# An LSTM with its weights made stationary: gates by units instead of rows, and the input part accumulated in PSUM

## The reference

```python
xW = jnp.einsum('ntd,dk->tnk', x, Wx) + b
c0 = jnp.zeros_like(h0)
def step(carry, xw_t):
    prev_h, prev_c = carry
    a = xw_t + prev_h @ Wh
    i = jax.nn.sigmoid(a[:, 0:Hdim])
    f = jax.nn.sigmoid(a[:, Hdim:2 * Hdim])
    o = jax.nn.sigmoid(a[:, 2 * Hdim:3 * Hdim])
    g = jnp.tanh(a[:, 3 * Hdim:4 * Hdim])
    next_c = f * prev_c + i * g
    next_h = o * jnp.tanh(next_c)
    return ((next_h, next_c), next_h)
_, hs = jax.lax.scan(step, (h0, c0), xW)
return x + jnp.transpose(hs, (1, 0, 2))
```

## Time and profile before

| | us |
|---|---|
| median of 3 runs | 1101.32 (1098.41 to 1105.87) |
| the profiled execution | 1104.56 |
| its span, from first to last instruction | 1102.8 |
| VectorE busy | 790.9 (72%) |
| TensorE products busy | 701.9 (64%) |
| TensorE weight loads busy | 578.7 (52%) |
| ScalarE busy | 550.2 (50%) |

### The profile page before, as it was taken

One profiled execution on the slowest core, in us unless ns is written; L12 is line 12 of the kernel. 1 busy time (PEld: TensorE's weight loads), 2 busy tenths in 40 slices (PEclk: granted clock), 3 DMA queues, 4 the chain that ended last, 5 costly groups with the idle time before them and its releaser, 6 DMA issues.

```text
span 1102.8 us, 88125 instructions
## 1 busy us (share of the span) xinstructions
PE 701.9 (64%) x36864; PEld 578.7 (52%) x36864; DVE 790.9 (72%) x4897; ACT 550.2 (50%) x3586; POOL 0.7 (0%) x6
## 2 busy tenths in 40 slices
PE   1766666666666666666666666666666666666664
PEld 1555555555555555545555555555555555555554
DVE  2676777777777767777767777777777777777776
ACT  0454555545555545555545555555555555455544
POOL 0000000000000000000000000000000000000000
PEclk9998999989999989999989999999999999899989
DMA  2000000000000000000000000000000000000000
GB/s 85 6 6 6 5 7 6 6 6 6 6 6 6 6 6 5 6 7 6 6 7 5 6 6 6 6 6 6 6 6 5 7 6 6 6 6 6 6 6 7
DMA packets 31869, 8.73 MB, mean 8 GB/s; under 512 B 31344, under 2 KB 31344, under 8 KB 31856
## 3 DMA queue, kind: packets, MB, share of 16 engines
q1 hardware_dynamic: 31248, 8.41, 3.2%
q10 hardware_dynamic: 608, 0.14, 0.1%
HBM read 6.43 MB, written 2.10 MB: 8 GB/s over the span
## 4 chain that ended last, share of the span: by engine, by line
DVE 50%; PE 25%; ACT 14%; issue 8%; DMA 2%; DVEq 1%; SPq 0%
DVE turned_bank L295 38%; PE gates L363 25%; DVE h_pad L313 8%; ACT tanh_o L211 8%; ACT turned_bank L214 6%; DVE scan_both L300 3%; DMA wh_raw<-in_L_cond_Wh_dram 2%; DVEq L329 1%; DVE cell L306 1%; DVE h_rows L269 0%; SPq L142 0%; SPq L137 0%; DVEq L268 0%; DVE wh L224 0%; DVE wh L221 0%
## 5 line engine op out<-in xcount | busy, mean ns | idle before, releaser
L363 PE MATMUL gates<-wh,h_pad 128*32 128x64 f32 x32768 | 594.7, 227 | 374.8 <-DVE h_pad L313 371.0
L363 PEld LDWEIGHTS gates<-wh,h_pad 128*32 128x32 f32 x32768 | 509.8, 114 | 489.1 <-DVE h_pad L313 485.1
L295 DVE STREAM_TRANSPOSE turned_bank<-gates 128x64 f32<-128x64 f32 x2048 | 478.5, 262 | 184.0 <-PE gates L363 170.8
L202 ACT ACTIVATE tanh_f<-turned_bank 128x8 f32<-128x8 f32 x512 | 90.7, 177 | 449.1 <-DVE turned_bank L295 417.5
L209 ACT ACTIVATE scan_both<-turned_bank 128x8 f32<-128x8 f32 x1024 | 185.1, 181 | 61.1 <-DVE turned_bank L295 19.7
L313 DVE SCALAR_TENSOR_TENSOR h_pad<-tanh_o,turned_bank 128x4 f32<-128x4 f32 x1024 | 132.8, 158 | 74.4 <-ACT turned_bank L214 5.2
L306 DVE TENSOR_TENSOR_SCAN cell<-scan_both 128x12 f32<-128x12 f32 x1024 | 143.8, 181 | 1.9 <-issue 0.3
L214 ACT ACTIVATE turned_bank<-cell 128x4 f32<-128x4 f32 x1024 | 143.3, 172 | 2.3 <-DVE cell L306 0.3
L345 PE MATMUL x_acc<-wx,x_units 128*32 128x128 f32 x2048 | 108.8, 287 | 16.6 <-DVE x_units L248 16.6
L211 ACT ACTIVATE tanh_o<-turned_bank 128x8 f32<-128x8 f32 x512 | 90.7, 177 | 29.2 <-DVE turned_bank L295 7.0
L215 ACT ACTIVATE half_d<-cell 128x8 f32<-128x8 f32 x512 | 100.4, 196 | 0.0
(11 more groups left out here) (24 smaller groups left out, 6.7 us busy)
## 6 DMA issues: line engine op xcount, KB each, us to landing
x_next<-in_x_dram SPq DMA_DIRECT2D x256, 8.0 KB
x_here<-in_x_dram SPq DMA_DIRECT2D x256, 8.0 KB
out_dram<-y_rows SPq DMA_DIRECT2D x256, 8.0 KB
wx_raw<-in_L_cond_Wx_dram SPq DMA_DIRECT2D x2, 512.0 KB
wh_raw<-in_L_cond_Wh_dram SPq DMA_DIRECT2D x2, 512.0 KB
bias_raw<-in_L_cond_b_dram ACTq DMA_DIRECT2D x4, 32.0 KB, 3.5
h_rows<-in_cond_dram ACTq DMA_DIRECT2D x4, 1.0 KB
```

The source lines that it names most:

```text
L202: nc.scalar.activation(tanh_f[:], of_step(BF, t), ACT.Tanh).then_inc(tanh_f_done, 1)
L295: nc.vector.transpose(turned[k], gates[k][:, 0:W]).then_inc(gates_turned[k], 1)
L363: last = nc.tensor.matmul(gates[k][q * R:(q + 1) * R, 0:W], h_stationary(b, t), wh[:, b, q, columns_of(k)], start=False, stop=b == M - 1, ...
```

## The change

The operands change places: the weights are stationary, 32 columns at a time, and the 4 columns of h move. A product's result has 32 units of one gate, half and quadrant as its partitions and the sequences as its columns. So the gates come out with units as partitions, the turns of the gate banks and the permuted copies of the weights are gone, and ScalarE reads the gate banks directly. A bank of one step consists of two parts (`PARTS`), each with its own stationary tiles.

The input part and the bias are written straight to the gate banks. There are two sets of four banks, each for 4 steps (`SET`). After the products of each step TensorE fills one bank of the other set: for each of the bank's two parts 4 products of the bias row with ones and 8 of `wx` with 16 columns of `x_units` (`x_part`). `x_acc`, `x_part` (the tile), `inject` and the identity go. The turn of the next `x` moves from step 2 to step 4 and waits for `x_used`. `tanh_c` moves from PSUM to SBUF. `BA`'s half 0 is now issued ahead of the wait for `h_done[1]`.

```diff
+    PARTS = (((F, 0), (F, 1)), ((G, 0), (I, 0)), ((G, 1), (I, 1)), ((O, 0), (O, 1)))
...
-        gates = [ps(f"gates{k}", [128, 512]) for k in BANKS]
-        x_acc = ps("x_acc", [128, 512])
-        turned_bank = [ps(f"turned_bank{k}", [128, 512]) for k in range(3)]
+        gates = [[ps(f"gates{s}{k}", [128, 512]) for k in range(len(PARTS))] for s in range(SETS)]
...
+        def group(t, k):
+
+            at = t % SET * N
+            return gates[t // SET][k][:, 0:2 * SC].rearrange("p (g c) -> p g c", g=2)[:, :, at:at + N]
...
-                    act.wait_ge(gates_turned[BF], now)
-                    nc.scalar.activation(tanh_f[:], of_step(BF, t), ACT.Tanh).then_inc(tanh_f_done, 1)
+                    act.wait_ge(gates_done[BF], now)
+                    nc.scalar.activation(tanh_f[:], group(t, BF), ACT.Tanh).then_inc(tanh_f_done, 1)
...
-                if ahead and t == 2:
-
+                if ahead and t == SET:
+                    dve.wait_ge(x_used, chunk + 1)
                     dve.wait_ge(x_next_loaded, (chunk + 2) * (Q * DMA))
                     nc.vector.transpose(x_units[:], x_next[:]).then_inc(x_turned, 1)
-                if ahead and t == STEPS - 1:
-                    make_x_part(chunk + 1)
-
-                def turn(k):
-                    dve.wait_ge(gates_done[k], now)
-                    nc.vector.transpose(turned[k], gates[k][:, 0:W]).then_inc(gates_turned[k], 1)
...
-                turn(BF)
-                turn(BA)
-                turn(BB)
                 forget()
-                turn(BO)
                 update(0)
                 update(1)
                 hidden(0)
...
+            def weights(w, b, gate, m, q):
+                at = gate * D + q * QD + m * R
+                return w[:, b, at:at + R]
+
+            def x_part(k, s):
+
+                for g, (gate, m) in enumerate(PARTS[k]):
+                    where = slice(g * SC, (g + 1) * SC)
+                    for q in range(Q):
+                        at = gate * D + q * QD + m * R
+                        nc.tensor.matmul(gates[s][k][q * R:(q + 1) * R, where], bias_row[:, at:at + R], ones[:],
+                                         start=g == 0, stop=False, tile_position=(0, q * R), skip_group_check=True)
+                    for b in range(M):
+                        for q in range(Q):
+                            last = nc.tensor.matmul(gates[s][k][q * R:(q + 1) * R, where], weights(wx, b, gate, m, q),
+                                                    x_units[:, b * R + s * SC:b * R + (s + 1) * SC],
+                                                    start=False, stop=False, tile_position=(0, q * R), skip_group_check=True)
+                return last
...
-                def recur(b, k):
-                    for q in range(Q):
-                        last = nc.tensor.matmul(gates[k][q * R:(q + 1) * R, 0:W], h_stationary(b, t),
-                                                wh[:, b, q, columns_of(k)], start=False, stop=b == M - 1,
-                                                tile_position=(0, q * R), skip_group_check=True)
+                def recur(b, k, parts=(0, 1)):
+                    for g in parts:
+                        gate, m = PARTS[k][g]
+                        for q in range(Q):
+                            last = nc.tensor.matmul(group(t, k)[q * R:(q + 1) * R, g, :], weights(wh, b, gate, m, q),
+                                                    h_units[:, b, (t - 1) % STEPS, :], start=False, stop=b == M - 1,
+                                                    tile_position=(0, q * R), skip_group_check=True)
                     return last
 
                 pe.wait_ge(h_done[0], now)
                 recur(0, BF)
+                recur(0, BA)
                 pe.wait_ge(h_done[1], now)
                 recur(1, BF).then_inc(gates_done[BF], 1)
...
+                recur(1, BA).then_inc(gates_done[BA], 1)
+                recur(0, BB)
+                recur(1, BB).then_inc(gates_done[BB], 1)
+                recur(0, BO)
+                recur(1, BO).then_inc(gates_done[BO], 1)
+                k, s = t % SET, (t // SET + 1) % SETS
+                if s == 1:
+                    last = x_part(k, 1)
+                    if k == SET - 1:
+                        last.then_inc(x_used, 1)
+                elif ahead:
+                    if k == 0:
+                        pe.wait_ge(x_turned, chunk + 2)
+                    x_part(k, 0)
```

More of the change, by code:

```diff
@@ L62, in lstm_residual_kernel @@
         x_here = sb("x_here", [128, QD])
-        x_part = sb("x_part", [128, GC])
         tanh_f = sb("tanh_f", [128, M, N])
         tanh_o = sb("tanh_o", [128, M, N])
+        tanh_c = [sb(f"tanh_c{m}", [128, N]) for m in range(M)]
         half_d = sb("half_d", [128, M, N])
@@ L102, in lstm_residual_kernel @@
         y_stored = sem("y_stored")
[L104 to L105 removed]
+        gates_done = [sem(f"gates_done{k}") for k in range(len(PARTS))]
         tanh_f_done = sem("tanh_f_done")
@@ L190, in _, with cell_tanh @@
                 act.dma_start(h0_rows[q * R:q * R + N, :], cond[:, q * QD:(q + 1) * QD]).then_inc(h0_loaded, DMA)
+            act.wait_ge(bias_zeroed, 1)
+            act.dma_start(bias_row[0:1, :], bias.rearrange("(a c) -> a c", a=1)).then_inc(bias_loaded, DMA)
             nc.scalar.activation(table_probe[:, 1:2], table_probe[:, 0:1], ACT.Tanh)
             act.wait_ge(zeroed, 2)
-            def of_step(k, t):
-                return turned[k].rearrange("p (g c) -> p g c", g=M)[:, :, t * N:(t + 1) * N]
+            def cell_tanh(m, now):
+                act.wait_ge(cell_done[m], now)
+                nc.scalar.activation(tanh_c[m][:], cell[:, m, :, K - 1], ACT.Tanh, scale=0.5).then_inc(tanh_done[m], 1)
             with act.Fori(0, T, STEPS) as t0:
@@ L218, in _, with scale_weights @@
         def _(dve):
[L219 to L228, removed]
+            def scale_weights(w, b, factor, loaded):
                 dve.wait_ge(loaded[b], DMA)
[L230 to L234, removed]
+                if factor != 1.0:
+                    nc.vector.tensor_scalar(w[:, b, G * D:], w[:, b, G * D:], factor, None, ALU.mult)
+                return nc.vector.tensor_scalar(w[:, b, 0:G * D], w[:, b, 0:G * D], 0.5 * factor, None, ALU.mult)
             nc.vector.memset(table_probe[:], 0.0)
@@ L338, in _ @@
         def _(pe):
-            def x_product(b, columns, chunk):
-                opens = (b, columns) == PIECES[0]
-                if opens:
-                    pe.wait_ge(x_turned, chunk + 1)
-                for q in range(Q):
-                    last = nc.tensor.matmul(x_acc[q * R:(q + 1) * R, columns], x_units[:, b * R:(b + 1) * R],
-                                            wx[:, b, q, columns], start=opens, stop=b == M - 1,
-                                            tile_position=(0, q * R), skip_group_check=True)
-                if (b, columns) == PIECES[-1]:
-                    last.then_inc(x_acc_done, 1)
@@ L351, in inject @@
-            def inject(k):
-                for q in range(Q):
-                    nc.tensor.matmul(gates[k][q * R:(q + 1) * R, 0:W], ident[:, q * R:(q + 1) * R],
-                                     x_part[:, columns_of(k)], start=True, stop=False,
-                                     tile_position=(0, q * R), skip_group_check=True)
+            def weights(w, b, gate, m, q):
[8 more added lines that the diff above has]
+                                         start=g == 0, stop=False, tile_position=(0, q * R), skip_group_check=True)
+                    for b in range(M):
+                        for q in range(Q):
[3 more added lines that the diff above has]
+                return last
```

119 lines of the change are left out of this document (39 added, 80 removed).

## The result

| | before | after |
|---|---|---|
| median, us | 1103.59 (4 runs, 1098.41 to 1109.97) | 2991.81 (4 runs, 2983.74 to 2998.10) |
| span of the profiled execution, us | 1102.8 | 2996.1 |

The changed kernel takes 2.7105 times as long (95% interval 2.6999 to 2.721). The forecast was 1715 us, with a range of 1000 to 1860: the direction and the mechanism were right, the size was far off.

The account below looks back on a forecast made before the run. Bound now: a serial recurrence, half the span VectorE. After: instruction fetches, 63 passes of 26.4 us (1663), last 8 steps 21, start 27, end 3: 1714, corrected to 1713, forecast 1715 us; range 1000 to 1860, its own 1420 to 1920.

Parts of the forecast that it names:

- What bounds the kernel, and what goes.: Whole kernel: a serial recurrence, half the span VectorE; all 2048 gate-bank turns, 478.5 us of VectorE, leave.
- I take 7 ns; the bounds are 6.7 and 14.: TensorE's 4-column products: time per load-and-multiply pair, taken from eight loads after a wait.
- At the 1.2 GHz level a product of 4 columns loses little, 10 us in all: TensorE's stretches at low clock: they were to add only 10 us to the changed kernel's time.
- 128r + 0.79: One recurrence step in us, r the time per pair: 1.69 us at 7 ns, 2.58 at 14.
- Rival 3: Recurrence products: no fetch trouble, but small products don't go below 14 ns; 1350 us, chance 0.18.
- 2070 us: Recurrence products: about 25 ns from product to product, 4 us a step; chance 0.03 within the 14 ns rival's.
- The body doesn't fit, and is fetched packet by packet, one ahead.: TensorE's loop: 2816 instructions, 11 packets, exceed its instruction memory; each packet is requested when the previous one is entered.
- A packet costs 2.2 us from request to arrival (bounds 1.84 and 2.9).: TensorE's instruction fetch: 1.2 us to the packet's start plus 0.96 us transfer; 11 packets make 24.2 us for 8 steps.
- today TensorE takes 4 us for 256 instructions, which hides it: Kernel before: executing one packet's instructions takes 4 us, longer than the 2.2 us claimed for a fetch.
- The jump back waits once more: End of TensorE's loop body: its target packet has been overwritten, adding 2.2 us, 26.4 us a pass.
- Rival 1: TensorE's loop: memory holds the whole body, or fetches run far enough ahead never to show; 900 us, chance 0.12.
- rival 2: TensorE's loop: fetches overlap, 0.96 us a packet, only the jump back waits 2.2 us; 1040 us, chance 0.18.

Follow-up runs that it names:

- the four-step body: Changed kernel's stationary weights with TensorE's loop body 4 steps instead of 8, whole computation kept: 1351.53 us, 1.2189 times before.
- the padded kernels: Kernel before with 16, 24 or 38 unread products a step added behind steps 0 to 6: 1360.32, 2089.16 and 2515.46 us.
- the two kernels with half of the contraction: Changed kernel without contraction half 0 in the recurrence: 2020.43 us; also without it in the x part, and without the bias: 988.91 us.
- the first three with fillers: Kernel with 4-step loop body plus unread products behind each step: 4 or 8 of 128 columns, or 8 of 256: 1278.00, 1206.96, 1404.81 us.

## Why the prediction was wrong in size and right in kind

- **What bounds the kernel, and what goes.** Right. The turns left VectorE, and its busy time fell by 338 us.
- **"I take 7 ns; the bounds are 6.7 and 14."** The value was wrong, the bound right: 13.4 ns in the changed kernel. I took it from the eight loads of the earlier trace rows. Their starts end at 504.29, and the ninth comes 53 ns later (the line below), so that row says nothing of the pace beyond eight, and I didn't look further. I asked what else could bind at that clock, but not whether the clock would stay. "At the 1.2 GHz level a product of 4 columns loses little, 10 us in all" is the sentence that failed. At 1.2 GHz a pair costs twice its time at that quick spacing, and the level lasts for the whole run. Even at 2.4 GHz it is 8.7 to 10 ns. In the changed kernel itself this cost little, since the fetches set its time.

```profile
504.34 0.84 PEld L363 LDWEIGHTS gates<-wh,h_pad 128*32 128x32 f32 x56
```

- **128r + 0.79.** Right where the products are last: 2.51 worked out, 2.48 measured in the four-step body. Rival 3, 1350 us with 14 ns and no fetches, gives that kernel's 1351.53 us, but by luck: what it called a floor of small products is the 1.2 GHz level. Its 2070 us weren't seen either: the pairs come 8.7 to 13.4 ns apart.
- **The body doesn't fit, and is fetched packet by packet, one ahead.** Right, and shown by the padded kernels and the four-step body: 827 packets where "in the hundreds (63 x 12)" was forecast. That it doesn't fit was a guess on the likelier half, and said so.
- **"A packet costs 2.2 us from request to arrival (bounds 1.84 and 2.9)."** This is the step that failed. It costs 3.8. I added the time up to the packet's start (1.2; 1.19 in the median, though I had only chosen it between 0.88 and 1.93) and its length (0.96, from one packet; 1.19), and took its end for the moment at which TensorE can go on. The trace of before couldn't show the third part, 1.4 us from the packet's end to the first instruction, since no one waited there; it should have stood in the bounds as an unknown with nothing to hide it. What TensorE does in these 1.4 us no run shows. 11 x 1.6 us a pass are 18 us, of the 20.3 by which a pass was underestimated (46.7 for 26.4). It also makes "today TensorE takes 4 us for 256 instructions, which hides it" a close thing: 4.0 against 3.8.
- **"The jump back waits once more", 2.2 us.** It is 4.4, as the packet behind the body is fetched first, in vain; and some 60 instructions after the jump the next boundary waits again. The Trainium skill, in the section named above, lets a taken branch whose target isn't in a window of two pages wait for a fetch. The changed kernel agrees. The kernel before doesn't: its jump goes back over 4.5 packets and fetched nothing in 63 passes.
- **The range.** With 3.8 in place of 2.2 the forecast's own sum gives 12 x 3.8 = 45.6 us a pass and 2940 us in all. Its named upper bound of 2.9 would have given 2250, and the range of 1420 to 1920 stopped at 2.5. The likeliest case was the true one, and its range was too narrow by its one term without an upper row.
- Rival 1 (900 us) and rival 2 (1040 us) are refuted: by the 827 packets, and by 3.8 us from packet to packet.

What isn't settled: why 8.7 to 10 ns and not 6.7 at 2.4 GHz; what fills the 1.4 us behind a packet's end; the memory's exact size, for which nothing between 1472 and 1612 instructions was tried; and what decides whether a pass of 1612 is fetched. The padded kernels, the two kernels with half of the contraction and the first three with fillers are one run each; their differences are far above the spread of the others.

## What to carry to other kernels

Count the instructions of a loop's body before anything else that multiplies them: an fp32 product is four (two loads, two multiplications). Up to 1472 and some waits the body was fetched once, from 1612 on again and again, and then 256 instructions cost 3.8 us if they would take less by themselves. Code behind the loop, which runs once, pays the same. Where an engine's queue never starves in the trace at hand, the price of starving isn't in that trace; bound it from above by something other than what is visible. And when products are made shorter, ask for the clock that TensorE will be granted then: durations of two widths give it, even where the clock view prints 1.00.

## What was not expected of the hardware

- TensorE, busy 93% of a span with products of 4, 16 and 32 columns, ran at 1.2 GHz to the end (194 ns for 4 columns). With 8 products of 128 columns more a step it ran at 2.4 GHz (173 ns), and 1351 us became 1207. With 4 it went to and fro.
- Work of that kind that nobody uses makes the kernel before 2.6% faster.
- A body at the memory's edge (1612 instructions) is fetched anew, with nine packets, in 17 of 62 passes and not at all in 45: 1360 us.
